# Flamingo layer with a routed FFN: first expert bias added by ACT from a column picked by register; output stores on ACT's queue, large transfers in pieces

## The reference

```python
x = x + tanh(g_xattn) * attention(layernorm(x), ctx, ctx, wq, wk, wv)
logits = layernorm(x) @ Wr + br              # 8 experts, the best 2 kept
gates  = softmax(logits of the best 2)
h      = relu(layernorm(x) @ W1[e] + b1[e])  # 128 -> 256
out    = sum over the 2 experts of gate * (h @ W2[e] + b2[e])
x = x + tanh(g_ffn) * out
```

## Time and profile before

| | us |
|---|---|
| median of 3 runs (lowest, highest) | 696.38 (696.27, 697.03) |
| the profiled execution | 698.32 |
| its span, first to last instruction | 696.6 |

### The profile page before, as it was taken

The page is one execution under the profiler, slowest core; times in us unless marked ns, Lnnn a source line. Parts: engine busy times, 40 slices in busy tenths (PEclk is TensorE's granted clock), DMA queues, the critical chain, the costliest instruction groups (busy, mean ns, idle before and its releaser), DMA issues.

```text
span 696.6 us, 18566 instructions
## 1 busy us (share of the span) xinstructions
PE 579.2 (83%) x6487; PEld 422.9 (61%) x6501; DVE 382.9 (55%) x1327; ACT 325.9 (47%) x592; POOL 271.1 (39%) x283
## 2 busy tenths in 40 slices
PE   0244877888898999998899997899999879999962
PEld 0112445555555677655677774677766767998852
DVE  7353455878777555577565568456455621343134
ACT  1112664556565555564455565356566334434320
POOL 4204000110460005566225444537177576272273
PEclk9995898789998999997999999899999999999995
DMA  8455637323444356454567643356333663567122
GB/s 136 104 133 167 168 87 209 79 62 91 112 106 105 79 96 136 121 151 90 112 101 176 134 128 89 89 116 169 98 100 78 108 159 107 109 144 129 44 68 73
DMA packets 157928, 79.45 MB, mean 114 GB/s; under 512 B 86464, under 2 KB 153664, under 8 KB 157488
## 3 DMA queue, kind: packets, MB, share of 16 engines
q1 hardware_dynamic: 139440, 58.17, 37.0%
q0 software_dynamic: 7168, 14.69, 8.7%
q10 hardware_dynamic: 11232, 5.40, 3.2%
HBM read 31.52 MB, written 36.76 MB: 98 GB/s over the span
## 4 chain that ended last, share of the span: by engine, by line
PE 61%; DMA 11%; DVE 10%; issue 7%; ACT 3%; SPq 3%; POOL 3%; POOLq 0%; DVEq 0%; ACTq 0%
PE y L600 11%; PE bank_oT L516 9%; PE scores L502 8%; PE max_scores L483 4%; DMA q_st<-q_dram 3%; PE hidden_p L583 3%; POOL back L1272 3%; PE hidden_p L584 3%; PE o L527 3%; PE hidden_p L585 3%; DVE neg_max L965 3%; PE hidden_p L586 2%; PE max_scores L538 2%; DMA q_dram<-q_hl 2%; PE group L461 2%
## 5 line engine op out<-in xcount | busy, mean ns | idle before, releaser
L965 DVE TENSOR_REDUCE neg_max<-max_scores 128x4 f32<-128x308 f32 x256 | 122.0, 477 | 171.1 <-PE max_scores L483 167.8
L727 ACT ACTIVATE probs<-scores 77x512 f32<-77x512 f32 x256 | 150.4, 596 | 73.4 <-PE scores L502 68.0
L1272 POOL DMA_INDIRECT back<-ys_dram,at x112 | 108.5, 968 | 72.2 <-issue 70.7
L483 PE MATMUL max_scores<-k_st,q_st 128*128 128x308 bf16 x256 | 83.5, 326 | 57.1 <-DVE neg_max L965 31.0
L1258 POOL DMA_INDIRECT xs_dram<-rows,at x112 | 109.9, 982 | 35.0 <-issue 35.0
L516 PE MATMUL bank_oT<-probs,v_cols 77*9 77x128 f32 x2048 | 108.4, 288 | 3.0 <-ACT probs L727 2.1
L502 PE MATMUL scores<-q_st,k_st 128*77 128x128 bf16 x1024 | 110.2, 235 | 0.9 <-issue 0.7
L502 PEld LDWEIGHTS scores<-q_st,k_st 128*77 128x77 bf16 x1024 | 77.6, 123 | 52.3 <-issue 47.0
L600 PE MATMUL y<-w_sb,hidden 128*128 x608 | 91.0, 292 | 0.0
L776 ACT ACTIVATE hidden<-hidden_p 128x512 f32<-128x512 f32 x76 | 45.4, 597 | 96.3 <-PE hidden_p L586 96.3
L600 PEld LDWEIGHTS y<-w_sb,hidden 128*128 128x128 f32 x608 | 81.4, 195 | 6.1 <-issue 2.5
(11 more groups left out here) (137 smaller groups left out, 927.1 us busy)
## 6 DMA issues: line engine op xcount, KB each, us to landing
ys_dram<-ys SPq DMA_DIRECT2D x38, 256.0 KB
q_st<-q_dram SPq DMA_DIRECT2D x16, 512.0 KB, 4.1
k_st<-k_dram SPq DMA_DIRECT2D x64, 77.0 KB, 3.8
xs_all<-x SPq DMA_DIRECT2D x16, 256.0 KB, 4.5
q_dram<-q_hl SPq DMA_DIRECT2D x16, 256.0 KB
xs_dram<-zeros_b ACTq DMA_DIRECT2D x2, 2048.0 KB, 13.3
out<-xs_all SPq DMA_DIRECT2D x16, 256.0 KB, 2.5
k_dram<-k_hl SPq DMA_DIRECT2D x48, 77.0 KB
```

Of the source, the lines that this page charges most:

```text
L483: mm(max_bank[:, 0:PER * KEYS], q_st[g % 3][:, h, seq_cut(b, S)], k_st[g % 3][:, h, b % NB, :, :].rearrange("p j k -> p (j k)"), start=Tru ...
L727: nc.scalar.activation(probs[h][:], score_bank[h % 2][0:KEYS, :], ACT.Exp, scale=SCALE).then_inc(s_exp, 1)
L965: V.tensor_reduce(neg_max[:, :, h, i], max_bank[:, 0:PER * KEYS].rearrange("p (j k) -> p j k", j=PER), AXIS_X, ALU.max, negate=True).then_ ...
L1272: G.indirect_dma_start(out=back[k][:, b % 16, :], out_offset=None, in_=ys_dram[c % 2][0:TILES[c] * 128, :], in_offset=bass.IndirectOffsetO ...
```

## The change

- PE: the matmul L583 goes (8 in a quad, 304 in all), with the register operation before it.
- ACT: relu of a half becomes four activations of 128 x 128, each with its bias from a column of `b1_cols` picked by a register; a register operation stands before each, and one load of four registers (`name_biases`) before each quad. DVE makes the column numbers (`tile_b`), one more operation for each chunk.
- ACT issues the store of the expert outputs (`store_y`), the zero and one planes at the start, the two weights in four pieces each (slots 22 to 29) and the clearing of `xs_dram` in eight pieces each (slots 14 to 21, 30 to 37). `b1_dram` and `b1_split` and their steps go; b2's rows are loaded in slot 5.
- SP: at r = 0 `store_k` stands between `store_max` and `stack_max`; loads of x and ctx move from the start of r = 0 to r = 1, behind `stack_k`; SP goes into its slots without the constants, for which `stack_k` waits now.
- DVE: the split of W1 moves to slots 33 and 34; late sums of gathered outputs come one slot later (95 to 97), with their stores.

```diff
-    SUM_AT = [GATHERED[b] + (1 if GATHERED[b] >= LAST_ATT else 4 + b % NB // 2) for b in range(SB)]
+    SUM_AT = [GATHERED[b] + (2 if GATHERED[b] >= LAST_ATT else 4 + b % NB // 2) for b in range(SB)]
...
                 if g < 3:
                     sp.wait_ge(s_kzero, g + 1)
+                    sp.wait_ge(s_const, 96)
...
             def slot(t):
                 u, r = t // NB, t % NB
-                if t == 10:
-                    sp.dma_start(w1_sb[:], w1).then_inc(s_w, 16)
-                    sp.dma_start(w2_sb[:], w2).then_inc(s_w, 16)
-                if r == 0 and group_on(u + 2):
-                    load_x(u + 2)
-                if r == 0 and u >= 2 and group_on(u):
-                    load_ctx(u)
+                if r == 0 and group_on(u - 3):
+                    store_max(u - 3)
+                if r == 0 and group_on(u - 1):
+                    store_k(u - 1)
+                if r == 0 and group_on(u - 3):
+                    stack_max(u - 3)
                 if r == 1 and group_on(u - 1):
                     stack_k(u - 1)
+                if r == 1 and group_on(u + 2):
+                    load_x(u + 2)
+                if r == 1 and u >= 2 and group_on(u):
+                    load_ctx(u)
...
-                for q in quads_at(t - 2):
-                    store_y(q)
...
-                        mm(o, b1_split[:, at_w], ones_b[:], start=True, stop=False, skip_group_check=True)
-                        mm(o, w_hi[:, at_w], tiles[:, 0, cut], start=False, stop=False, skip_group_check=True)
+                        mm(o, w_hi[:, at_w], tiles[:, 0, cut], start=True, stop=False, skip_group_check=True)
...
+            def name_biases(q):
+                c = CHUNK_OF_QUAD[q]
+                at_tile = 4 * (q - QUAD0[c])
+                if at_tile == 0:
+                    act.wait_ge(s_rt, ROUTE * (c + 1))
...
+                _, held[q] = nc.values_load_multi_w_load_instructions(
+                    tile_b[c % 2][0:1, at_tile:at_tile + 4], engines=[mybir.EngineType.Activation], min_val=0,
...
-                nc.scalar.activation(hidden[:, k % 4, :, :, :].rearrange("p t m s -> p (t m s)"), hidden_bank[:],
-                                     ACT.Relu).then_inc(s_relu, 1)
+                for i in range(2):
+                    for m in range(HC):
+                        j = i * HC + m
+                        last = nc.scalar.activation(
+                            hidden[:, k % 4, i, m, :], hidden_bank[:, j * 128:(j + 1) * 128], ACT.Relu,
+                            bias=b1_cols[:, bass.ds(held[q][2 * half + i] + m, 1)])
+                last.then_inc(s_relu, 1)
...
-                if t in (15, 19):
-                    act.wait_ge(s_zeros, 1)
-                    act.dma_start(xs_dram[t // 19].rearrange("(t p) w -> p t w", p=128),
-                                  zeros_b[:, None, 0:2 * D].to_broadcast([128, TMAX, 2 * D])).then_inc(s_clear, 16)
+                if t == 5:
+                    act.dma_start(b2_rows, b2.partition_broadcast(96)).then_inc(s_bias, 16)
+                if 14 <= t < 22 or 30 <= t < 38:
+                    i, part = t // 30, TMAX // 8 * 128
+                    first = part * (t - (14, 30)[i])
+                    act.dma_start(xs_dram[i][first:first + part, :].rearrange("(t p) w -> p t w", p=128),
...
+                if 22 <= t < 30:
+                    part = E * HID // 4
...
                 if active(ob):
                     output_rows(ob)
+                for q in quads_at(t - 2):
+                    store_y(q)
...
                 for q in quads_at(t):
+                    name_biases(q)
                     relu(q, 0)
...
+            act.wait_ge(s_zeros, 1)
+            for i in range(2):
+                act.dma_start(k_dram[i][:, 3, :, :], zeros_b[0:ROWS, None, 0:KEYS4].to_broadcast([ROWS, HG, KEYS4])
+                              ).then_inc(s_const, 16)
+                act.dma_start(q_dram[i][:, 3, :], zeros_b[:]).then_inc(s_const, 16)
...
-                if t in (20, 21):
-                    split_experts(t - 20)
+                if t in (33, 34):
+                    split_experts(t - 33)
```

More of the change, by code:

```diff
@@ L94, in flamingo_kernel @@
     DENSE_AT = [GATED_ALL + 1 + n for n in range(DENSE // NB * E)]
-    STORE_AT = [SUM_AT[NB * g + NB - 1] + 1 for g in range(G0)] + [DENSE_AT[E - 1] + 2, DENSE_AT[2 * E - 1] + 2]
+    STORE_AT = [SUM_AT[NB * g + NB - 1] + 2 for g in range(G0)] + [DENSE_AT[E - 1] + 2, DENSE_AT[2 * E - 1] + 2]
     SLOTS = max(STORE_AT) + 1
@@ L190, in flamingo_kernel @@
         tile_w = [sb(f"tile_w{i}", [128, TMAX], I32) for i in range(2)]
+        tile_b = [sb(f"tile_b{i}", [128, TMAX], I32) for i in range(2)]
         xsT = [sb(f"xsT{i}", [128, 2, 512], BF16) for i in range(3)]
@@ L211, in flamingo_kernel @@
         flat = "p a b -> p (a b)"
-        b1_rows, b1_rest = (back[k][:].rearrange(flat)[0:96, :] for k in range(2))
         b2_rows, b2_rest = (rows[k][:].rearrange(flat).bitcast(F32)[0:96, 0:E * D] for k in range(2))
@@ L231, in flamingo_kernel @@
         s_bias = sem("biases_loaded")
[L232 removed]
+        s_b1c = sem("b1_columns_loaded")
         s_const = sem("constant_planes_stored")
@@ L364, in load_tiles @@
                                  transpose=True).then_inc(s_xs[q % 3], 16)
[L366 to L374, removed]
             def store_out(g):
@@ L384, in slot @@
                 u, r = t // NB, t % NB
-                if t == 10:
-                    sp.dma_start(w1_sb[:], w1).then_inc(s_w, 16)
-                    sp.dma_start(w2_sb[:], w2).then_inc(s_w, 16)
-                if r == 0 and group_on(u + 2):
-                    load_x(u + 2)
-                if r == 0 and u >= 2 and group_on(u):
-                    load_ctx(u)
+                if r == 0 and group_on(u - 3):
[4 more added lines that the diff above has]
+                    stack_max(u - 3)
                 if r == 1 and group_on(u - 1):
                     stack_k(u - 1)
+                if r == 1 and group_on(u + 2):
+                    load_x(u + 2)
+                if r == 1 and u >= 2 and group_on(u):
+                    load_ctx(u)
+                if r == 2 and group_on(u - 1):
+                    store_q(u - 1)
                 if r == 3 and group_on(u - 1):
                     stack_q(u - 1)
-                for q in quads_at(t - 2):
-                    store_y(q)
[L398 to L404, removed]
                 for g in range(NG):
@@ L769, in rows_high @@
                 copy(rows[c % 2][:, i:i + NB, 0:D], xn2[:]).then_inc(s_rhi, 1)
+            held = {}
+            def name_biases(q):
[3 more added lines that the diff above has]
+                    act.wait_ge(s_rt, ROUTE * (c + 1))
+                if q == 0:
+                    act.wait_ge(s_b1c, 16)
+                _, held[q] = nc.values_load_multi_w_load_instructions(
+                    tile_b[c % 2][0:1, at_tile:at_tile + 4], engines=[mybir.EngineType.Activation], min_val=0,
+                    max_val=(E - 1) * HC, skip_runtime_bounds_check_because="DVE clamps the expert's number to 0..7")
             def relu(q, half):
@@ L783, in outputs, with store_y @@
                 copy(ys[q % 2][:].rearrange("p t d -> p (t d)"), y_bank[:]).then_inc(s_ys, 1)
+            def store_y(q):
+                c = CHUNK_OF_QUAD[q]
+                act.wait_ge(s_ys, q + 1)
+                if q == QUAD0[c] and c >= 2:
+                    for g in range(SEQ0[c - 2] // NB, SEQ0[c - 1] // NB):
+                        act.wait_ge(s_back[g], 16 * 2 * NB)
+                first = 512 * (q - QUAD0[c])
+                act.dma_start(ys_dram[c % 2][first:first + 512, :].rearrange(
+                    "(t p) w -> p t w", p=128), ys[q % 2][:]).then_inc(s_yst[q % 2], 16)
             def gap_exponent(c):
@@ L871, in slot @@
                     gap_exponent(NC)
+            act.wait_ge(s_zeros, 1)
[3 more added lines that the diff above has]
+                act.dma_start(q_dram[i][:, 3, :], zeros_b[:]).then_inc(s_const, 16)
             act.dma_start(gates_in[:, 0:1], g_xattn.partition_broadcast(128)).then_inc(s_gin, 16)
             act.dma_start(gates_in[:, 1:2], g_ffn.partition_broadcast(128)).then_inc(s_gin, 16)
-            act.dma_start(b1_dram.rearrange("(m p) -> p m", p=128), b1, allow_slow_non_contiguous=True).then_inc(s_b1d, 16)
+            act.wait_ge(s_const, 64)
+            act.wait_ge(s_ones, 1)
+            for i in range(2):
+                act.dma_start(k_dram[i][::4, 3, :, :].rearrange("p h n -> p (h n)"), ones_k[:]).then_inc(s_const, 16)
             act.dma_start(wr_sb[:], w_router).then_inc(s_bias, 16)
```

59 lines of the change are left out of this document (23 added, 36 removed).

## The result

The changed kernel takes 713.22 us (median of 707.23, 713.22 and 714.68) against 696.38: 1.022 of the kernel before, 95% interval 1.013 to 1.031. The forecast was 691.1 in a range of 676 to 706, so the time lies above the range, on the side of the 0.30. The profiled execution is the one of 713.22, span 711.5. An execution more than 1.5% above the fastest of its kernel counts as slow and is left out of every ratio, and since the profiled one of the experiment s1_max_first is such a one, no time or clock is read from its trace.

A forecast was written before the change was run, and what follows sets the result against it. It took key and query transfers through DRAM to bound the start, PE and DVE turns the attention slots, and PE the quad slots. Terms -18.1 + 11.8 + 0.4 - 18.6 + 20.4 - 1.2 = -5.3 gave 691.1 us, range 676 to 706.

The forecast's parts named there:

- the 0.30: The chance the prediction gave to the changed kernel being slower.
- SP's start: SP no longer waits for the constants, so the first keys are stored at about 13 us: gain 6.6 us.
- Weights and clears in pieces: Early query transfers no longer wait behind weight loads and 2 MB clears: gains 5.1, 3.7 and 2.7 us.
- step 3: `stack_max` behind `store_k` in SP's queue delays `scores` of new groups: cost 11.8 us, ends 1 and 16.
- W1's split: The split moves to two other slots and the pieces meet query transfers in slots 22 to 37: together +0.4 us.
- The bias: Taking b1 off PE gains 18.6 us in full slots; the relu in four on ACT takes back 20.4.
- step 6: Relu in four on ACT ends 0.60 us later per half, where PE has little or no room: cost 20.4 us.
- C: Slower, about 706 to 714 us: ACT's four activations do not overlap, pitch 0.41, 23 us more; chance 0.30.
- Stores on ACT at nothing: Output stores add some 0.6 us of issue on ACT per quad slot, within 3 us of room: no effect.
- The end: After the last gathers, one dense sum goes ahead of the last routed sums: -1.2 us.
- A: Better cover, about 678 us: key stores do not hold up the maxima, ACT's pitch under 0.2 us; chance 0.20.

The follow-up runs named there:

- s1_max_first: The changed kernel with the stacking of the maxima put back ahead of SP's three key stores: 0.980 of the kernel before.
- s7: The kernel before with the start only (constant planes from ACT, w_att ahead of ctx, weights and clears in pieces, W1's split at slots 33, 34): 0.976 of before.
- s2: The kernel before with the stacking of the maxima moved behind SP's three key stores: 1.031 of before.
- s4: The kernel before with the bias moved off PE and the relu in four: 1.007 of before.
- s12: s7 with the y stores issued by ACT instead of SP, sums and output stores a slot later: 0.984 of the kernel before.
- s11: The changed kernel with the stacking of the maxima behind one key store instead of three, in SP's queue: 0.990 of the kernel before.
- s10: The changed kernel with the stacking of the maxima issued by POOL once the low half of k is there: 0.980 of the kernel before.
- s3: The changed kernel with the bias matmuls, `b1_split` and the relu of 512 columns put back: 1.021 of the kernel before.
- s5: The changed kernel with maxima stacked ahead of the key stores and the bias matmuls with one relu put back: 0.983 of the kernel before.
- s9: s7 with PE's output matmuls moved behind the first half of the next four tiles in slots 77 to 80: 0.975 of the kernel before.
- s6: s1_max_first with PE's output matmuls behind the next four tiles' first half in all slots without attention, dense ones included: 0.981 of the kernel before.
- s8: s1_max_first with PE's output matmuls moved behind the next four tiles' first half only in slots 77 to 80: 0.979 of the kernel before.

## Why the prediction was wrong, step by step

1. *SP's start* was right in size: 6.0 us at slot 8 against 6.6. But the keys are stored at 15.02 and not at about 13, and only 2.3 us of it come with the bias left on PE (s7).
2. *Weights and clears in pieces* were right: 11.2 us ahead at slot 20, where the prediction looked for some 12 with the late maxima paid, and s7 shows 17 us (12 to 22) for steps 1, 2 and 4 together against 18.1 - 0.4.
3. ***`stack_max` behind `store_k`* is the step that failed.** It was right in the direction and in the place, and mis-sized: 11.8 with an upper end of 16, measured 22 (s2) and 29 (s1 against the change). Two things were wrong in it. The landing was put at 5.0 us after the first key store, since by the earlier trace rows the keys themselves had landed at 5.45. But the maxima stand behind all three and need their own way after them: 6.3 in the median. That is 1.3 us in each of 14 groups, 18 us, where the first 5.0 had used up the cover. It had not everywhere: in slots 49 and 61, where step 3 had nothing, PE waited 2.8 and 2.5 us. And the late end was cut at 16 by the same wrong bound; nothing in the rows excluded a landing behind the keys. With 6.3 the step gives about 30, more than s2's 22: part is made up in the next slot (slot 25 went from 7.63 to 6.96).
4. *W1's split:* within s7, not to be told from nothing.
5. and 6. *The bias* was right in its parts (368 ns, pitch 0.257) and in its net: +1.8, with s4 at 1.4 to 8. The way to the net was not. PE waits 9.1 us before `rows_out` in 13 places (about 15 in some 30 were forecast) and 7.2 for half 0's relu in 5. Before it was 2.2 and 3.8, so the waits grew by 10.3 us where step 6 had 17.5 (12.0 + 1.7 + 3.8): up to slot 71 only 7 slots show a wait before `rows_out`, of 0.33 to 0.63 us, where the prediction had counted eleven rooms of zero and 0.60 us in each. What step 6 lacked is the clock from slot 71 to slot 82: in six kernels with relu in four it averages 0.78 to 0.86 there, in the seven with one relu 0.93 to 1.00. Two terms stood on no row: by the slope of rows 9 an activation of 128 columns takes 262 ns and not 277 (597 - 384 x 178/204), and the 0.04 us that C adds for a register operation doesn't show in the measured pitch.
7. *Stores on ACT at nothing:* open, between nothing and 0.7% (s12).
8. *The end:* 42.6 us from the last y copy to the end, before 43.2. That is -0.6 instead of -1.2.

With step 3 at 22 to 29 in place of 11.8, the sum is +5 to +12 and the time 701 to 708. The 5 us from there to 713 may be the clock from slot 71 on, or the spread of the runs (707.23 to 714.68); no run changed the clock alone. The forecast gave slower 0.30 by rival C, whose mechanism (a pitch on ACT of 0.30 or more) did not happen. That the time fell where C had put it is luck: it came mostly by step 3. A was wrong too: the maxima were held up. No rival carried the late end of step 3 further than 16.

## What to carry to other kernels

A small transfer that PE waits for belongs ahead of bulk in its queue: here one moved line cost 22 to 29 us. Issued behind only the first of three stores, from the same queue or from another, it cost PE 6 to 7 us of waiting instead of 35. When a transfer is moved behind n others, price it as landing after the last of them plus its own way, not with them, and set that against the room. A kernel that does five things at once hides a gain: the start alone was worth 2.4% and the whole lost 2.2%.

## What the runs showed of the hardware

- A 32 KB transfer issued behind three stores of 77 KB was used 3.6 to 4.8 us after its own issue (14 groups of the changed kernel); behind one, in the same queue, 2.7 to 3.4 (six groups of s11); from POOL's queue, mostly behind one, it landed in 2.9 (s10).
- An activation of 128 x 128 with a bias column addressed by register takes 368 ns and starts 0.257 us after the one before. An estimate from the figures of the Trainium skill (ScalarE: Activation LUTs, What ACT_TABLE_LOAD costs) is 387 and 294; the measured values are shorter, and what the register operation between costs doesn't show apart from that.
- From the y copy of slot 71 to that of slot 82 the mean granted clock splits the kernels by relu, one profiled execution each: 0.98 (before), 0.93, 0.95, 0.95, 0.93, 0.98 and 1.00 (s2, s3, s5, s7, s9, s12) with one relu and the bias matmuls, 0.85 (the changed kernel), 0.84, 0.84, 0.86, 0.86 and 0.78 (s4, s6, s8, s10, s11) with relu in four. In the changed kernel PE runs 53 matmuls fewer there and waits 12.4 us for relu instead of 6.0. The waits alone don't explain the clock: s8 and s6 wait 4.7 and 3.7 us, less than the kernel before, and stay at 0.86 and 0.84. That the missing matmuls lower it is a guess that fits; no run took them away without the relu in four.
